# Row maxima a whole sequence ahead of the scores, and the last ranks behind expert block 2

## The reference

```python
q, k, v = (src @ W + b for each)            # 16 heads of 8 features
scores = einsum('bqhd,bkhd->bhqk', q, k) * scale
probs = softmax(scores)                     # needs the row maxima of the scores
x = layer_norm(src + (probs @ v) @ Wo + bo)
keys = (x @ router_w + router_b)[..., 0]
expert_idx = remainder(floor(keys), 4)
for e in range(4):
    y = relu(x @ W1[e] + b1[e]) @ W2[e] + b2[e]
    ff_out += where(expert_idx == e, y, 0)
return layer_norm(x + ff_out)
```

## Time and profile before

| | before |
|---|---|
| median of three runs | 1255.11 us |
| profiled execution, its own time | 1262.19 us |
| span of that execution | 1259.0 us |
| PE busy | 1073.6 us (85%) |
| DVE busy | 971.7 us (77%) |
| ACT busy | 790.1 us (63%) |
| POOL busy | 630.8 us (50%) |
| granted clock of PE, mean | 0.931 |
| chain that ended last: PE, DVE, issue, POOL | 33%, 27%, 10%, 7% |
| its largest line | DVE L1407, 22% |

### The profile page before, as it was taken

One profiled execution on the slowest core, in us unless ns is written; L12 is line 12 of the kernel. 1 busy time (PEld: TensorE's weight loads), 2 busy tenths in 40 slices (PEclk: granted clock), 3 DMA queues, 4 the chain that ended last, 5 costly groups with the idle time before them and its releaser, 6 DMA issues.

```text
span 1259.0 us, 21070 instructions
## 1 busy us (share of the span) xinstructions
PE 1073.6 (85%) x6007; PEld 405.5 (32%) x6007; DVE 971.7 (77%) x2221; ACT 790.1 (63%) x1670; POOL 630.8 (50%) x1077
## 2 busy tenths in 40 slices
PE   4978989559998999899998998998989888879992
PEld 3755445212222222222222222222222222334440
DVE  7527777148999999899899899898998981366774
ACT  2413233103988878878878888888888787335550
POOL 6513343322235745735745745646546344575765
PEclk9997787555999999999999999999999999989996
DMA  5000000044224234234234234144143205365540
GB/s 155 10 0 1 0 0 0 17 84 102 68 37 102 81 59 102 73 67 103 69 70 102 60 73 106 43 82 101 44 97 90 50 11 168 83 213 163 166 131 15
DMA packets 101874, 94.36 MB, mean 75 GB/s; under 512 B 23101, under 2 KB 93182, under 8 KB 101768
## 3 DMA queue, kind: packets, MB, share of 16 engines
q1 hardware_dynamic: 94968, 80.19, 27.2%
q0 software_dynamic: 5504, 12.73, 2.8%
q10 hardware_dynamic: 1296, 0.20, 0.1%
HBM read 50.83 MB, written 42.92 MB: 74 GB/s over the span
## 4 chain that ended last, share of the span: by engine, by line
PE 33%; DVE 27%; issue 10%; POOL 7%; ACT 2%; SPq 1%; DMA 1%; POOLq 0%; ACTq 0%; DVEq 0%
DVE a_mx L1407 22%; PE ps_o L995 12%; PE ps_x L973 10%; POOL out L1551 6%; PE ps_s L980 4%; PE ps_m L954 2%; PE ps_m L938 2%; ACT a_prob L1066 1%; DVE a_attn L1315 1%; DVE a_stats L1351 1%; PE ps_m L932 1%; DVE a_stats L1365 1%; DVE x_tok L1346 1%; PE ps_m L951 1%; ACT a_a_t L1080 1%
## 5 line engine op out<-in xcount | busy, mean ns | idle before, releaser
L1407 DVE TENSOR_REDUCE a_mx<-ps_x 128x1 f32<-128x512 f32 x1024 | 641.8, 683 | 65.1 <-PE ps_x L973 60.5
L1066 ACT ACTIVATE a_prob<-ps_s 128x512 f32<-128x512 f32 x1024 | 543.7, 604 | 90.5 <-PE ps_s L980 83.5
L973 PE MATMUL ps_x<-ks,a_qs 48*128 48x512 bf16 x1024 | 342.6, 397 | 72.7 <-DVE a_mx L1407 57.5
L980 PE MATMUL ps_s<-a_qs,ks 50*128 50x512 bf16 x1024 | 329.4, 386 | 8.1 <-ACT a_prob L1066 7.6
L995 PE MATMUL ps_o<-a_prob,vaug 128*32 128x512 f32 x2048 | 273.5, 606 | 0.0
L973 PEld LDWEIGHTS ps_x<-ks,a_qs 48*128 48x128 bf16 x1024 | 74.5, 94 | 387.7 <-DVE a_mx L1407 311.6
L1161 POOL CAST a_mx_parts<-a_mx 128x32 bf16<-128x32 f32 x32 | 6.6, 206 | 213.8 <-PE ps_m L936 167.8
L1551 POOL DMA_INDIRECT out<-vaug,e_ids x76 | 84.6, 1113 | 21.7 <-issue 21.7
L980 PEld LDWEIGHTS ps_s<-a_qs,ks 50*128 50x128 bf16 x1024 | 73.0, 93 | 41.6 <-ACT a_prob L1066 37.7
L1186 POOL DMA_INDIRECT rows<-a_row,a_pos_i x64 | 64.2, 1003 | 28.6 <-issue 15.6
L995 PEld LDWEIGHTS ps_o<-a_prob,vaug 128*32 128x32 f32 x2048 | 40.3, 108 | 74.4 <-issue 47.0
(11 more groups left out here) (247 smaller groups left out, 1596.8 us busy)
## 6 DMA issues: line engine op xcount, KB each, us to landing
stacks<-a_parts SPq DMA_DIRECT2D x192, 128.0 KB, 2.4
a_qs<-stacks SPq DMA_DIRECT2D x64, 192.0 KB, 4.6
ks<-stacks SPq DMA_DIRECT2D x64, 192.0 KB, 4.6
x_tok<-rows SPq DMA_DIRECT2D x19, 520.0 KB, 4.1
rows<-vg_t SPq DMA_DIRECT2D x7, 520.0 KB
a_qk<-in_L_ffn_W SPq DMA_DIRECT2D x13, 256.0 KB
a_z<-in_L_ffn_W SPq DMA_DIRECT2D x7, 256.0 KB
a_z_t<-in_L_ffn_W SPq DMA_DIRECT2D x6, 256.0 KB
```

Source lines behind the costliest of these rows:

```text
L973: pe.matmul(ps_x[:, bank(b, n), :], qs[b % 2][own, pair, qt * P:(qt + 1) * P], ks[b % 2][own, pair, :], start=True, stop=True).then_inc(mx ...
L980: pe.matmul(ps_s[:, bank(i, n), :], ks[r][own, pair, kt * P:(kt + 1) * P], qs[r][own, pair, :], start=True, stop=True).then_inc(qk_mm, 1)
L1066: act.activation(prob[:, (s // 2) % RING, u % 4, :], ps_s[:, bank(i, u), :], ACT.Exp, scale=SCALE).then_inc(exp_done, EXP_STEP)
L1407: dve.tensor_reduce(mx[:, half, col:col + 1], ps_x[:, bank(b, n), :], AX.X, ALU.max)\
```

## The change

1. `BEHIND` and `maxima_at` are gone. Body i makes all 64 maxima units of sequence i + 1, so body -1 has 64 and body 15 none.
2. In `MISC`, "mx1" stands at slot 6 (was 9) and "mx0" at slot 21 (was 24).
3. On POOL, `split_maxima(i + 1, 0)` stands in front of L1250 (was behind L1255).
4. `dve_block(0)` stands in body 16 in front of the router's steps, and `pool_rstd(0)` in the middle of POOL's router chain of body 16.
5. The rank step of sequence 15 (body 17) stands behind expert block 2 on PE (was behind block 1). On POOL its four indirect DMAs are sent as two and two, around `pool_out(1)`.
6. `dve_late` is cut in four: `dve_counts` before block 2, and three pieces inside blocks 2, 4 and 5, between the variance and the wait for `pool_rstd`; the running sums `dve_ends` are in block 3. SP waits for the last ranks before block 8 (was 6).

```diff
-    MISC = (("rk", 1, -2), ("vg", 3, 2), ("v", 4, 1), ("ob", 5, -1), ("at", 8, -1), ("mx1", 9, 0), ("z", 11, 2),
-            ("wo", 13, -1), ("q", 15, 2), ("k", 17, 2), ("mx0", 24, 1), ("oa", 29, 0))
+    MISC = (("rk", 1, -2), ("vg", 3, 2), ("v", 4, 1), ("ob", 5, -1), ("mx1", 6, 0), ("at", 8, -1), ("z", 11, 2),
+            ("wo", 13, -1), ("q", 15, 2), ("k", 17, 2), ("mx0", 21, 1), ("oa", 29, 0))
...
-                if j == 6:
+                if j == ex.EARLY - 1:
                     sp.wait_ge(scattered, 16 * T * B)
                     ex.sp_pad_ends(sp)
...
-                    b, first = maxima_at(i, s)
-                    if 0 <= b < B:
-                        if first == 0:
-                            wait(pe, st0_in, STACKS * (b + 1))
-                        if first == UNITS // 2:
-                            wait(pe, st1_in, STACKS * (b + 1))
+                    if on(i, 1):
+                        if s == 0:
+                            wait(pe, st0_in, STACKS * (i + 2))
+                        if s == SLOTS // 2:
+                            wait(pe, st1_in, STACKS * (i + 2))
...
             ex.pe_layer2(pe, 0)
             ex.pe_block(pe, 1)
+            ex.pe_block(pe, 2)
             body(B + 1, (B + 1) % 2)
-            for j in range(2, ex.NB):
+            for j in range(3, ex.NB):
                 ex.pe_block(pe, j)
...
+                if on(i, 1):
+                    split_maxima(i + 1, 0)
                 if on(i, 2):
...
-                if on(i, 1):
-                    split_maxima(i + 1, 0)
...
+                    if i == B:
+                        ex.pool_rstd(pool, 0)
...
-            ex.pool_rstd(pool, 0)
             ex.pool_block(pool, 1)
-            body(B + 1, (B + 1) % 2)
-            for j in range(2, ex.NB):
+            ex.pool_rstd(pool, 2)
+            find_places(B - 1)
+            send_rows(B - 1, range(0, T // 2))
+            ex.pool_out(pool, 1)
+            ex.pool_rstd(pool, 3)
+            send_rows(B - 1, range(T // 2, T))
+            ex.pool_out(pool, 2)
+            for j in range(4, ex.NB):
                 ex.pool_block(pool, j)
...
+                    if i == B and s == ROUTE // 2:
+                        ex.dve_block(dve, 0)
...
-            ex.dve_block(dve, 0)
             ex.dve_block(dve, 1)
             body(B + 1, (B + 1) % 2)
             dve.wait_ge(misc_free, used(B + 1, "rk"))
-            ex.dve_late(dve)
-            for j in range(2, ex.NB):
+            ex.dve_counts(dve)
+            ex.dve_block(dve, 2, ex.dve_late_filled)
+            ex.dve_block(dve, 3, ex.dve_ends)
+            ex.dve_block(dve, 4, ex.dve_late_experts)
+            ex.dve_block(dve, 5, ex.dve_late_rows)
+            for j in range(6, ex.NB):
                 ex.dve_block(dve, j)
```

78 lines of the change are left out of this document (43 added, 35 removed).

## The result

The changed kernel takes 1273.5 us (median of four runs, 1269.9 to 1277.5) against 1255.3 us before: ratio 1.016, 95% interval 1.011 to 1.021. It is slower by 18.2 us where 13.1 less was predicted. Its profiled execution took 1272.55 us, span 1270.5, mean clock 0.921.

What follows compares the result with a forecast made beforehand. DVE and PE, both near their limit, were taken to hold each other through three banks. Terms +11.3, -8.6, +0.3, -1.6 and -14.5 sum to -13.1 us, giving 1242 us on the median; range 1230 to 1261.

Steps and rivals of the forecast that it cites:

- I take it that PE reaches L954 0.25 us earlier: Bodies 3 to 13: "mx1" moved from slot 9 to 6 lets PE start L954 0.25 us sooner, so r_in is ready sooner.
- POOL's L1219 and DVE's L1358 shutting each other out: Bodies 3 to 13: r_in waits because L1219 starts first; being ready 0.72 us ahead of L1219 would remove the wait.
- The 1.03 us a body: Bodies 3 to 13: difference between body 7 and body 2, expected back without r_in's wait; part of the -8.6 us.
- Rival A: Bodies 3 to 13: r_in still waits and the split only costs, +0.5 us in 11 bodies; 1256 us, chance 0.25.
- Here there are four, so I take no wait: Slot 0 of full bodies: with four requests in flight, not eight, the stacks come in time, costing nothing.
- Rival B: Slot 0 of each of 15 bodies: stacks come late and PE stops; at 2 us a body 1272 us, chance 0.08.
- bodies 0 to 2: First three bodies: the split in front of L1250 costs +0.3 us, with no wait to remove.
- The split in front of L1250: Bodies 3 to 13: splitting the maxima earlier on POOL delays ACT's L1102 and the exponentials, 0.5 us a body.
- "mx0" at slot 21: Bodies 3 to 13: moving it from slot 24 shifts 0.24 us of PE and is worth nothing.
- Body -1: Ahead of the full bodies: ten more maxima products 5.7, "vg" and "v" 3.2, wait for stacks 2.4; sum +11.3 us.
- Body 15, -1.6: Last attention body: ten maxima products fewer, about 0.17 us of PE each, give 1.6 us; bounds 0 and 6.
- Expert stage, -14.5: Experts: ranks pass without a wait and block 8 starts 15.9 us earlier, less 1.4 us for POOL and DVE overlapping.

Runs made afterwards that it cites:

- tail_end: tail with POOL's L1219 moved to the end of its body: 1260.5 us, ratio 1.006 to the kernel before.
- ahead62: The changed kernel with the maxima 62 units ahead instead of 64: 1242.4 us, ratio 1.002 to the kernel before.
- ahead62s: The changed kernel 62 units ahead, with the split back behind L1254 and "mx0" back at slot 24: 1242.3 us, ratio 1.011 to the kernel before.
- tail: The kernel before with only the expert part (items 4 to 6): 1232.7, 1230.2 and 1232.6 us on three chips, ratios 1.005, 0.999 and 0.992.
- before: The kernel without the change, first profile: median 1255.3 us.
- before_b: The kernel without the change, profiled again on chip 3: 1256.3 us, where the kernel before has 1254.9.
- tail_vg: tail with POOL's L1219 moved in front of the ranks and their indirect DMAs: 1232.3 us, ratio 0.986 to the kernel before.
- after: The changed kernel with all six items, first profile: 1273.5 us, ratio 1.016 to the kernel before.
- ahead62_b: The changed kernel 62 units ahead, run a second time on chip 9: 1259.7 us, ratio 1.003 to the kernel before.
- split_back: The changed kernel, still 64 units ahead, with the split behind L1254 and "mx0" at slot 24: 1253.9 us, ratio 1.025 to the kernel before.
- copies_back: split_back with POOL's two copies for the router's rows moved behind L1258: 1265.4 us, ratio 1.013 to the kernel before.

## Why the prediction was wrong, step by step

- **"I take it that PE reaches L954 0.25 us earlier": wrong in sign.** "wo" ended 15.39 us after x_tok and not 15.26; in slot 6 "mx1" found no spare time, PE got 0.12 us later there.
- **"POOL's L1219 and DVE's L1358 shutting each other out": wrong, and the failure that matters.** The 1.03 us a body that the forecast gave back hung on it. Two rows that stand beside each other (a wait that ends 0.88 us into L1219) were taken for cause, and body 7 hid what speaks against it. In ten of the eleven bodies of the same trace DVE is already late at the reductions ahead of r_in. Its last reductions ahead of r_in, then r_in, in body 3, where x_tok starts at 449.00:

```profile
463.43 1.29 DVE L1407 TENSOR_REDUCE a_mx<-ps_x 128x1 f32<-128x512 f32 x2 [0.61 <-PE ps_x L973]
465.66 0.69 DVE L1358 TENSOR_TENSOR a_r_in<-vg_t,ps_m 128x512 f32<-128x512 f32 x1 [0.95 <-PE ps_m L954]
```

```profile
464.74 1.28 POOL L1219 TENSOR_TENSOR vg_t<-a_z,rows_b 128x512 f32<-128x512 f32 x1
```

The product of this reduction had ended 13.96 us after x_tok, it starts at 14.43 (13.99 in body 7), and L1219 comes 1.31 us behind that. By the rule cited from the Trainium skill (SBUF — State Buffer, section "Who interferes with whom") L1219 was not the holder, and tail_end agrees (16.57 us with L1219 at 38). Rival A happened: the wait stayed in all eleven bodies, r_in at 16.5 to 16.6 us, and bodies 3 to 13 took 9.2 us more and not 8.6 less.
- **"Here there are four, so I take no wait": wrong.** With four requests in flight the last took 5.3 to 5.5 us in the full bodies, as 5.62 with eight. The first request, placed at 34.4 to 35.8 us after x_tok, came at 35.7 to 37.4. The bound was in the text (42.7 against slot 0 at 41.3); I took the favourable side of it. Rival B happened in part: 3.2 us over eleven bodies, not one wait in each, and by ahead62 little of it would come back with the stops gone. Of the 2.3 us in bodies 0 to 2, where +0.3 was taken, 1.5 are such stops.
- **The split in front of L1250**: 0.5 taken, 0.33 in slots 22 to 24; right in kind. "mx0" at slot 21 was taken as nothing and costs 0.10; ahead62s gives both back together, 0.40 us a body (on another chip than ahead62).
- **The clock was not in the sum at all.** 4.0 us in bodies 3 to 13 and 6 in body 15. I read the full clock of rows 1 as given, though no row told how much more idle time it bears. Without these 10 us the changed kernel would be at about 1263.5 us (an estimate from the two figures), near the end of the range.
- **Body -1**: waits and jobs to 0.3 us. +9.67 for +11.3: from the first maxima product on it is +10.85, with 5.0 for the ten maxima where 5.7 was taken, and that product starts 1.2 us earlier behind x_tok.
- **Body 15, -1.6**: ten products fewer gave 0.7.
- **Expert stage, -14.5: right**, -13.7, at the places named, though 1 to 2 us of it are not the part's own.
- **The range** had 1261 as its end because A's and B's losses were never added together. The same trace spoke for A and left B undecided.

## What to carry to other kernels

Where two engines hold each other at the full clock, a small loss can cost the clock on top: here bodies 0.3 us longer had falls of 0.7 to 1.2 us more in some of them. That the 0.3 us is the cause is likely and not shown. Before a wait is put down to the instruction that it ends beside, look for the same delay in all rounds and on instructions ahead of it, and then move that instruction away. Running a stage further ahead costs its start-up once and the slack of its inputs in every round: here one slot of slack (62 and not 64 units) took away the stops and 3.7 us of the start-up, but the bodies got no shorter, and the part that paid (the experts) was independent of it. A wait that goes by the chip can be larger than the change one measures: compare kernels on one chip.

## What the hardware showed

- The same bodies took 47.2 us on three chips (tail on 14, 4 and 11) and 48.5 on one or two others (before and before_b), by a wait of 1.3 us at one DVE instruction. Where it is, a reduction that reads only PSUM also starts late just ahead of it in ten of eleven bodies of both kernels (14.34 to 14.55 us after x_tok and not 13.99), though its product had ended at 13.96; in tail_vg it doesn't. The wait is never there in bodies 1 and 2. What holds DVE stays open.
- The granted clock fell to 1.2 GHz for 3.4 us, or two or three times that, in kernels whose bodies without a stop take 48.8 to 48.9 us (after, ahead62_b, tail_end; after has shorter ones behind stops), in before and before_b with 48.5 never, and in split_back and copies_back only at stops for the stacks of over 1 us. A fall of 3.4 us costs 0.7 to 1.2 us.
- One otherwise useless product a slot in PE's gaps kept the full clock in body 15 in three profiles, where it takes 40.8 to 41.0 us, 0.5 to 0.7 us more than the 40.3 of the kernel before.
